# Rotary turn ahead of the root mean square division, with new instruction orders, in a fused transformer block

## The reference, cut to what matters

```python
q = (x @ Wq.T).reshape(bsz, seqlen, H, HD)...      # H = 16 heads of HD = 16
k = (x @ Wk.T).reshape(bsz, seqlen, KVH, HD)...    # KVH = 4
v = (x @ Wv.T).reshape(bsz, seqlen, KVH, HD)...
q = _rms_norm(q)      # v * rsqrt(mean(v * v) + EPS), over each head's 16 channels
k = _rms_norm(k)
q = _apply_rotary(q, cos, sin)   # (v1*cos + v2*sin, -v1*sin + v2*cos), v1, v2 halves of a head
k = _apply_rotary(k, cos, sin)
q = q * q_gain
...                   # scores in a window of 64, softmax, times v, mix of head pairs, Wo
```

## Time and profile before

| what | value |
|---|---|
| median of 3 runs | 3313.47 us (3312.93 to 3314.41) |
| the profiled execution's own time | 3308.83 us |
| its span in the trace | 3306.9 us |
| PE matmul busy | 3088.1 us, 93% |
| PE weight load busy | 2456.8 us, 74% |
| DVE busy | 2398.5 us, 73% |
| ACT busy | 1788.9 us, 54% |
| POOL busy | 545.9 us, 17% |
| mean granted TensorE clock | 0.969 |

### The profile page before, as it was taken

One profiled execution on the slowest core, in us unless ns is written; L12 is line 12 of the kernel. 1 busy time (PEld: TensorE's weight loads), 2 busy tenths in 40 slices (PEclk: granted clock), 3 DMA queues, 4 the chain that ended last, 5 costly groups with the idle time before them and its releaser, 6 DMA issues.

```text
span 3306.9 us, 79649 instructions
## 1 busy us (share of the span) xinstructions
PE 3088.1 (93%) x27330; PEld 2456.8 (74%) x27330; DVE 2398.5 (73%) x5990; ACT 1788.9 (54%) x3585; POOL 545.9 (17%) x1164
## 2 busy tenths in 40 slices
PE   3789999999999999999999999999999999999977
PEld 2567777777777777777777777777777777777755
DVE  4567777777777777777777777777777777777754
ACT  1255555565555565555565555566554556555554
POOL 0012111112111112111112111112111111111111
PEclk9899999999999999999999999999999999999998
DMA  1000000000000000000000000000000000000000
GB/s 60 8 10 16 15 2 15 13 15 15 15 2 15 13 15 15 15 2 15 13 15 15 15 8 9 13 15 15 15 15 2 13 15 15 15 15 2 14 10 16
DMA packets 42084, 44.86 MB, mean 14 GB/s; under 512 B 2608, under 2 KB 41392, under 8 KB 42032
## 3 DMA queue, kind: packets, MB, share of 16 engines
q1 hardware_dynamic: 42032, 44.20, 4.4%
HBM read 21.12 MB, written 16.78 MB: 11 GB/s over the span
## 4 chain that ended last, share of the span: by engine, by line
PE 77%; issue 8%; DVE 6%; ACT 4%; POOL 4%; DMA 0%; POOLq 0%; SPq 0%; DVEq 0%; ACTq 0%
PE Q L364 14%; PE HID L414 13%; PE Y L435 13%; PE Q L555 8%; PE HID L372 4%; PE Q L823 4%; PE Q L593 3%; PE Q L588 3%; PE Q L757 2%; PE Q L606 2%; PE Q L837 2%; PE Q L733 1%; ACT a_qz L1123 1%; PE Q L762 1%; PE Q L570 1%
## 5 line engine op out<-in xcount | busy, mean ns | idle before, releaser
L435 PE MATMUL Y<-w2t,f_hh 128*128 128x256 f32 x2048 | 550.9, 302 | 72.5 <-DVE f_hl L1307 72.3
L949 ACT ACTIVATE f_r<-HID,b1c 128x512 f32<-128x512 f32 x512 | 350.9, 685 | 327.8 <-PE HID L414 240.9
L435 PE MATMUL Y<-w2t,f_hl 128*128 128x256 f32 x2048 | 519.5, 286 | 0.0
L435 PEld LDWEIGHTS Y<-w2t,f_hh 128*128 128x128 f32 x2048 | 395.0, 193 | 141.8 <-DVE f_hl L1307 83.8
L1307 DVE TENSOR_TENSOR f_hl<-f_r,f_hh 128x512 fp32r<-128x512 f32 x512 | 351.6, 687 | 188.1 <-ACT f_hh L950 185.8
L414 PE MATMUL HID<-ff_xh,w1t 128*128 128x512 f32 x1024 | 448.9, 438 | 14.8 <-DVE ff_xl L1299 14.8
L414 PE MATMUL HID<-ff_xl,w1t 128*128 128x512 f32 x1024 | 419.5, 410 | 0.0
L435 PEld LDWEIGHTS Y<-w2t,f_hl 128*128 128x128 f32 x2048 | 397.1, 194 | 4.2
L1409 DVE TENSOR_TENSOR a_s<-Q,cst 128x512 f32<-128x512 f32 x512 | 329.3, 685 | 76.6 <-PE Q L555 68.9
L950 ACT ACTIVATE f_hh<-HID,b1c 128x512 fp32r<-128x512 f32 x512 | 351.9, 687 | 0.0
L1123 ACT ACTIVATE a_qz<-Q 128x512 f32<-128x512 f32 x512 | 279.1, 602 | 46.8 <-PE Q L762 46.5
(11 more groups left out here) (186 smaller groups left out, 7048.4 us busy)
## 6 DMA issues: line engine op xcount, KB each, us to landing
x<-in_x SPq DMA_DIRECT2D x32, 512.0 KB, 4.2
out<-x SPq DMA_DIRECT2D x32, 512.0 KB, 3.0
b_vm<-b_v SPq DMA_DIRECT2D x64, 96.0 KB, 2.1
a_s<-in_w SPq DMA_DIRECT2D x1, 1024.0 KB, 8.0
a_qz<-in_w SPq DMA_DIRECT2D x1, 1024.0 KB, 10.2
a_s<-in_w_qkv SPq DMA_DIRECT2D x1, 768.0 KB, 4.7
cst<-in_const SPq DMA_DIRECT2D x1, 389.0 KB, 5.6
a_qT<-in_w_b SPq DMA_DIRECT2D x1, 384.0 KB, 5.9
```

Of the source, the lines that this page charges most:

```text
L435: mm = pe.matmul(Y[t // 2][:, (t % 2) * D:(t % 2 + 1) * D], h[:, fb % 2, t * P:(t + 1) * P], w2t[:, fb, :], start=False, stop=(fb == FB - ...
L949: act.activation(f_r[:, fb % 2, :], HID[fb % 2][:], ACT.Relu, bias=b1c[:, fb:fb + 1]).then_inc(f_rr, 1)
```

## The change

**The arithmetic of B.** `cosines(t)` and `sines(t)` now read the raw projection, `rotate(t)` adds them, and `norm_qk(t)` multiplies the turned values by the reciprocal root, as the last of the four. The instructions, their number and their shapes stay; what each waits for changes: the cosines and sines wait for `raw(b, t)` alone, `rotate` for both, `norm_qk` for `rotate` and the roots, and ScalarE's `stack_hi` for `norm_qk`.

**The orders.** The lists of PE, ACT, DVE and POOL are all new, in both phases. One semaphore wait of `turn_qk(3, 0)` holds in all cases now. The core of the diff (the orders of phase 2, each list of calls written as a line instead of one call a line):

```diff
+                    def cosines(t):
+                        dve.wait_ge(b_raw_s, j + 1)
+                            dve.wait_ge(b_qr_s, j - 1)
+                        dve.tensor_tensor(b_qn[:, t % 2], b_raw[:, t].rearrange(...), table("cos", t, 0, HD), ALU.mult)
+                    def rotate(t):
+                        dve.tensor_tensor(b_qn[:, t % 2], b_qn[:, t % 2], b_rsn[:, t % 2], ALU.add).then_inc(b_rot, 1)
+                    def norm_qk(t):
+                        dve.wait_ge(b_rs_s, b * 2 + min(t, 1) + 1)
+                        dve.wait_ge(b_rot, j + 1)
+                            dve.wait_ge(b_lo, j - 1)
+                        dve.tensor_tensor(b_qr[:, t % 2], b_qn[:, t % 2], b_rs[:, t, :]..., ALU.mult).then_inc(b_qr_s, 1)
 # GpSimd, sines(t)
-                        pool.wait_ge(b_qn_s, j + 1)
-                            pool.wait_ge(b_qr_s, j - 1)
+                        pool.wait_ge(b_raw_s, j + 1)
+                            pool.wait_ge(b_rot, j - 1)
 # GpSimd, order of phase 2
-  squares(0) squares(1) squares(2) norm_rstd(ff) sines(0) squares(3) sines(1) sines(2) sines(3) norm_rstd(at) norm_rstd(ff)
+  sines(0) squares(0) sines(1) squares(1) squares(2) squares(3) sines(2) norm_rstd(ff) sines(3) norm_rstd(at) norm_rstd(ff)
 # VectorE, order of phase 2, its head
-  sums(0) roots(0) norm_qk(0) sums(1) cosines(0) sums(2) rotate(0) low(5) sums(3) stack_lo(0) roots(1) norm_qk(1) low(6)
-  cosines(1) rotate(1) own_apply() stack_lo(1) low(7) norm_qk(2) cosines(2) norm_qk(3) own_norm_lo() rotate(2)
+  sums(0) cosines(0) roots(0) rotate(0) sums(1) norm_qk(0) cosines(1) sums(2) low(5) stack_lo(0) sums(3) low(6) roots(1)
+  rotate(1) norm_qk(1) own_apply() stack_lo(1) low(7) cosines(2) cosines(3) rotate(2) norm_qk(2) own_norm_lo()
 # TensorE, order of phase 2, its head
-  up(5) up(6) down(4) down(5) turn_qk(0, 0) up(7) turn_qk(0, 1) turn_qk(0, 2) scores(0) down(6) scores(1) own_norm()
-  turn_qk(1, 0) turn_qk(1, 1) down(7) turn_qk(1, 2) numer(0) numer(1) scores(2) up(0) turn_numer(0)
+  up(5) down(4) up(6) up(7) turn_qk(0, 0) turn_qk(0, 1) down(5) turn_qk(0, 2) down(6) scores(0) scores(1) own_norm()
+  turn_qk(1, 0) turn_qk(1, 1) down(7) turn_qk(1, 2) numer(0) numer(1) scores(2) up(0) turn_numer(0)
 # TensorE, the rest of phase 2
-  up(1) scores(3) numer(2) down(0) turn_y(0) turn_qk(2, 0) turn_qk(2, 1) numer(3) turn_qk(2, 2) project(0) down(1) scores(4)
-  turn_numer(1) turn_qk(3, 0) up(2) turn_y(1) numer(4) scores(5) project(1) turn_qk(3, 1) turn_qk(3, 2) numer(5)
-  next_norm(0) scores(6) up(3) next_norm(1) turn_numer(2) numer(6) down(2) turn_y(2) scores(7) up(4) project(2) numer(7)
+  up(1) scores(3) turn_y(0) turn_qk(2, 0) numer(2) turn_qk(2, 1) turn_qk(2, 2) project(0) down(0) numer(3) up(2)
+  turn_qk(3, 0) turn_numer(1) scores(4) down(1) turn_qk(3, 1) turn_y(1) scores(5) numer(4) turn_qk(3, 2) project(1)
+  scores(6) numer(5) up(3) next_norm(0) turn_numer(2) scores(7) down(2) next_norm(1) turn_y(2) down(3) numer(6) numer(7)
```

More of the change, by code:

```diff
@@ L1156, in phase2 @@
                     exps(1)
+                    own_norm()
                     evacuate(1, 0)
                     evacuate(1, 1)
-                    own_norm()
                     evacuate(1, 2)
+                    stack_hi(2)
                     evacuate_numer(0)
@@ L1460, in phase1 @@
                         return
+                    phi(0)
                     low(5)
-                    phi(0)
+                    phi(1)
                     own_apply()
-                    phi(1)
                     phi(2)
@@ L1647, in phase2 @@
                     sums(0)
+                    cosines(0)
                     roots(0)
+                    rotate(0)
+                    sums(1)
                     norm_qk(0)
-                    sums(1)
-                    cosines(0)
+                    cosines(1)
                     sums(2)
-                    rotate(0)
                     low(5)
+                    stack_lo(0)
                     sums(3)
-                    stack_lo(0)
+                    low(6)
+                    roots(1)
@@ L1657, in phase2 @@
+                    rotate(1)
+                    norm_qk(1)
+                    own_apply()
                     if guarded:
                         maxima(0)
-                    roots(1)
-                    norm_qk(1)
-                    low(6)
-                    cosines(1)
-                    rotate(1)
-                    own_apply()
-                    stack_lo(1)
+                    stack_lo(1)
+                    low(7)
+                    cosines(2)
+                    cosines(3)
@@ L1666, in phase2 @@
+                    rotate(2)
+                    norm_qk(2)
                     if guarded:
                         maxima(1)
-                    low(7)
-                    norm_qk(2)
-                    cosines(2)
-                    norm_qk(3)
                     own_norm_lo()
-                    rotate(2)
                     finish_second(s)
+                    stack_lo(2)
                     if guarded:
                         maxima(2)
-                    cosines(3)
-                    low(0)
+                    normalise(0)
@@ L1679, in phase2 @@
+                    rotate(3)
                     if guarded:
                         maxima(3)
-                    normalise(0)
-                    stack_lo(2)
+                    y_lo(0)
+                    low(0)
+                    norm_qk(3)
+                    residual(0)
+                    stack_lo(3)
                     low(1)
-                    rotate(3)
-                    y_lo(0)
                     next_stats()
-                    residual(0)
+                    normalise(1)
```

257 lines of the change are left out of this document (128 added, 129 removed).

## The result

The changed kernel takes 3281.4 us (median of 4 runs, 3279.8 to 3285.97), the kernel before 3313.2 us on the same chip (4 runs, 3311.26 to 3314.41): a ratio of 0.9907 (95% interval 0.989 to 0.9924), 32 us faster. I had forecast 3332 us and gave "faster" a third. So the sign was wrong, though the time lies in the range that I gave (3262 to 3372).

The account below looks back on a forecast made before the run. PE was taken to bound the kernel, busy 97%, so only its gaps could be won. Head +0.8, tail -0.2 and phase 1 0 gave +0.6 us a step, +19 us over 31 steps: 3332 us, range 3262 to 3372.

Parts of the forecast that it names:

- VectorE's path to `own_norm`: Phase 2 head, from `stack_lo(0)` through `own_apply`: 5.6 us, reaching `own_norm` at 1579.3, as before.
- `stack_lo(0)` at 7.1 us after `up(5)`: Phase 2 head: `stack_lo(0)` ends at 1573.65, from 6.6 us of VectorE work plus 2.6 us of contention.
- the walk: VectorE's head, turn by turn against GpSimd's squares and sines: five calls or steps lose 2.7 us, taken as 2.6.
- The serial work: VectorE alone from `sums(0)` through `stack_lo(0)`, without contention: 6.6 us, of which `roots(0)` 2.3.
- PE's path: Phase 2 head: about 3.0 us of transposes and `down` calls, then `scores(0)` to `own_norm` staying 2.67; `own_norm` at 1579.4.
- The clock, +0.8: Phase 2 head: half clock over `down(5)` and `down(6)` could delay `own_norm`; +0.8 us taken between -0.1 and +1.4.
- The tail, -0.2: Rest of phase 2: one fewer run of partial-array matmuls on PE saves 0.2 us a step.
- Phase 1, +0: Phase 1: same calls, 11 runs in both orders, no gap before; 0 us, bounds -0.2 to +0.3.
- the signs that I named: Head, if right: lengthened rows, PE gap over 3 us, half clock over `down(5)` and `down(6)`, `own_norm` 13.6 us or more after `up(5)`.
- Those for "wrong": `stack_lo(0)` ended 5.4 us or less after `up(5)`, steps with clock 1.00, a loop step under 98 us.
- Faster, little contention: Rival, chance 0.33: head contention stays 0.9 us; 3248 us, or 3295 with a low clock stretch.
- Slow handover: Rival, chance 0.05: VectorE and GpSimd handovers in the head cost 0.7 us more a step; 3353 us.

Follow-up runs that it names:

- e6: Changed kernel with the four squares of a sequence moved from GpSimd to ScalarE: 3218.89 us, ratio 0.9716 to the kernel before.
- e3: Changed kernel with `down(6)` moved back between `scores(0)` and `scores(1)` on PE: 3280.62 us.
- e8: Changed kernel with `low(5)` and `stack_lo(0)` ahead of `cosines(1)` on VectorE and `down(5)` ahead of `turn_qk(0, 0)` on PE: 3275.13 us.
- e1: Changed kernel with phase 1's lists put back to the old order on every engine: 3281.67 us.
- e5: Changed kernel, turn still on raw values, with GpSimd's old order, the FFN norm's root ahead of the sines: 3347.24 us.
- e4: Changed kernel with the old arithmetic (`norm_qk` first, then the turn) and GpSimd's old order, under the new lists of PE, ScalarE and phase 1: 3331.51 us.
- e2: Changed kernel with the tail of phase 2 put back to the old order on all engines, new head kept: 3317.17 us.
- e10: Kernel before, with its own arithmetic and head of phase 2, given the new orders of phase 1 and the tail: 3319.83 us.
- e11: Kernel before with the squares moved from GpSimd to ScalarE, nothing else changed: 3249.92 us, ratio 0.9811.
- e12: Changed kernel with squares on ScalarE and GpSimd's root of the FFN's norm ahead of all sines: 3273.55 us.
- e9: Changed kernel with squares on ScalarE, `low(5)` and `stack_lo(0)` ahead of `cosines(1)`, and `down(5)` ahead of `turn_qk(0, 0)`: 3221.10 us.

## Why the prediction was wrong

The forecast was +0.6 us a step; the step measured -1.13. What failed is the time of `stack_lo(0)`, forecast 0.8 us later than before and measured 0.1 earlier, and with it VectorE's path to `own_norm`. By the forecast's own terms:

1. **`stack_lo(0)` at 7.1 us after `up(5)`, the step that failed.** The mechanism, contention on the raw turn's rows, was right; two terms were too large. *The contention:* line 1591 and the root steps did lengthen (the cosine products stand on line 1581 now), in the order of the walk 0.17, 0.51, 0.47, 0.53, 0.30 where it had 0.3, 0.65, 0.65, 0.7, 0.4. That is 1.98 us, where I took 2.6. *The serial work:* it was 6.3, not 6.6: 8.28 - 1.98 in the changed kernel; e6, with 0.57 lost, gives 6.86 - 0.57 = 6.3 again. I had read 2.3 us for `roots(0)` off the old order, and 0.3 of it was VectorE waiting for its own last result: line 1582 starts 0.37 us behind the last root step there [0.19 of it idle, rows 4], `rotate(0)` 0.10 behind it now, since it needs no root. Together 8.3 instead of 9.2, so `stack_lo(0)` ends 6.20 us after `up(5)` (before 6.30), and PE idles 2.4 us, not 3.35.
2. **VectorE's path to `own_norm`: "as before" was wrong.** The 0.9 us of item 1 go straight through: from the end of `stack_lo(0)` to `own_apply` it is 4.3 us, where the forecast's terms give 4.2. `own_apply` starts at 10.47 us after `up(5)`, in the mean, before 11.38: 0.9 earlier. Only 0.55 of it reach `own_norm`, since `own_apply`'s own first half is slower now (1.09 instead of 0.74 us, beside GpSimd's sines). The forecast also let `own_norm` wait for all of `own_apply`, where it needs the first half, and it compared the result with 1579.54, the `own_norm` of a step with a low stretch (12.98 us after `up(5)`); at full clock that was 12.15.
3. **PE's path: "it stays 2.67" was wrong, and made up for.** With `down(6)` out of it, `scores(0)` to `own_norm` is 2.39 us at full clock. In the changed kernel both paths arrive together: PE doesn't wait at `own_norm`, while in e3 and e8, where PE is there sooner, it waits 0.12 and 0.80 us and starts at the same 11.6. That is the time of VectorE's path, where the forecast's paths had 12.7 and 12.8 (1579.3 and 1579.4 less 1566.56).
4. **The clock, +0.8.** Of the forecast's +0.8 the paths were -0.1 and the rest was for a longer gap that exposes more of a stretch at the lower level. The gap grew by 0.2 us only, 18 of 28 steps have a stretch of 3.4 us where before 26 had one of 3.4 or 6.8, and the cost in the mean stayed 0.7.
5. **The tail, -0.2.** I counted one run of partial-array matmuls less, at 0.2. It is -0.48. The runs in the tail did fall from 9 to 8, but the order also has one passage from `numer` to `scores` less (0.31 us from start to start, against 0.21 the other way round), and `numer(7)` now stands behind `numer(6)` without a full matmul between. Start to start, the tail's passages into, out of and between such runs take 5.00 us before (20 of them) and 4.33 after (18); the two pairs that stand in their place take 0.18. That is the -0.48; the rest of the tail takes as long as before. Phase 1, +0: right (e1; -0.1 in the table).

The rows of the kernel before on which the sum up to `own_apply` rests besides:

```profile
1576.28 0.79 DVE L1591 TENSOR_TENSOR a_s<-a_s,cst 128x320 f32<-128x320 f32 x1
1577.53 0.49 DVE L1597 TENSOR_TENSOR a_s<-a_s 128x320 f32<-128x320 f32 x1 [0.46 <-POOL a_s L1779]
```

So -0.55 up to `up(0)` (17.90 to 17.35 in the mean, 17.21 to 16.65 at full clock), -0.48 in the tail and -0.1 in phase 1 stand for the +0.8, -0.2 and 0 of the sum. Of the signs that I named, the lengthened rows and the gap ahead of line 733 came, and a lower clock there in 18 of 28 steps; but the gap is not over 3 us, and `own_norm` is 12.54 us behind `up(5)` and not 13.6. Those for "wrong" came in two of three: steps at full clock, and a mean step under 98 us.

No rival was right as put. "Faster, little contention" has the sign, but wanted 0.9 us of contention and less than 1.8 to decide; it was 2.0. "Slow handover" doesn't show: `cosines(1)` ends at 1657.42, its own 0.48 before that is 1656.94, and the square beside it ends at 1657.07, so nothing is lost behind the other's end; so it is in the other long rows.

What I had weighed too low is what VectorE gets in return, up to `own_apply`. It no longer waits for sines (0.67 us ahead of `rotate(0)` and 0.46 ahead of `rotate(1)` before) and waits 0.3 us less for its own last results around the roots, for 0.8 us more contention (1.98, against 0.44 + 0.45 and 0.31 of `cosines(1)` before). The calls ahead of `own_apply` are the same fifteen in both orders. e5 brings a wait for sines back (1.90 us), at 66 us. Taken alone the contention with the squares costs a lot, as e6 shows with 62 us, the clock's part included. What share of e4's 50 us belongs to the arithmetic and what to GpSimd's order was not told apart.

## What to carry to other kernels

When a reorder trades a wait for contention, work out both in the same list: the idle time that goes, and the lengthened rows that come, up to each of the calls that another engine waits for, and not only up to the first. A tail saving found under one head may be eaten by waits under another (e2, e10), so it is to be checked against the waits there, on each engine's list. And when rows of VectorE are several times their usual length beside GpSimd's, try ScalarE for GpSimd's part before any new order, if ScalarE has room (it is busy for 55% here): four instructions a step moved were worth twice the whole change.

## What the runs showed of the hardware

- Root steps with one SBUF operand (lines 1549 and 1551, 128x20) took 0.69 and 0.65 us beside GpSimd's squares, and 0.17 and 0.18 in e6 without them. The first two instructions of `own_apply` (line 1293, 128x256) took 0.59 and 0.58 us beside sines and 0.41 in the kernel before. The reduction of line 1539 took 0.47 to 0.49 everywhere. The Trainium skill, page SBUF - State Buffer, section "Who interferes with whom", has such a `tensor_scalar` contend if it runs in a two-port mode, and a reduction never; the rows agree with both, while the mode itself is not to be seen in them.
- A passage out of partial-array matmuls is uneven: the first full matmul starts 0.21 us after the last one of `scores`, but 0.31 after the last one of `numer`, where full matmuls of 256 columns follow one another in 0.12. The Trainium skill, page TensorEngine Tiling (Array Packing), section "Key Properties", says that a change of the mode drains the engine, with no figure.
- The lower clock (0.50, that is 1.2 GHz) came mostly behind PE's gap at the head: in none of 28 steps with a longest wait near 1 us (e6, e11), in 17 and 18 with 2.3 and 2.4 us (e12, changed kernel), in all with 3.9 (e5). But the kernel before had it in 26 with 2.1 us and e2 in all with 2.4. And e8 and e9, whose longest wait in a step is 0.8 us, ahead of `own_norm`, had it in 16 and 3 steps, with the stretch starting 11.3 us or more after `up(5)`. So the length of the wait alone doesn't decide it; what else does stays open.
